# One row tile of every sixteenth pair fetched by SyncE, row by row, in a graph network kernel

## The reference

```
x = layernorm(x + three_graph_convolutions(x, src, dst))
bf  = exp(coeff * (dist[:, None] - centers[None, :]) ** 2)
bf  = ssp(ssp(bf @ W1 + b1) @ W2 + b2)
msg = h[src] * edge_feat * bf * cut[:, None]
agg = segment_prod(msg, dst)
x = layernorm(x + ssp(agg @ W3 + b3))
```

## Time and profile before

| what | value |
|---|---|
| median of 3 runs | 3990.79 us (3990.15 to 3992.11) |
| the profiled execution | 3993.41 us |
| its span, from first to last instruction | 3991.6 us |
| PE busy | 3243.2 us (81%) |
| DVE busy | 3237.0 us (81%) |
| ACT busy | 2862.5 us (72%) |
| POOL busy | 1935.5 us (48%) |

### The profile page before, as it was taken

How to read it: one execution, slowest core, us unless ns; L and a number is a source line. 1 busy time by engine, 2 the same in 40 slices (tenths; PEclk the granted TensorE clock), 3 DMA queues, 4 the chain that set the end, 5 groups by cost and what they waited for, 6 DMA issues and landing times. The chain is left out here.

```text
span 3991.6 us, 61034 instructions
## 1 busy us (share of the span) xinstructions
PE 3243.2 (81%) x21477; PEld 2658.1 (67%) x21477; DVE 3237.0 (81%) x5053; ACT 2862.5 (72%) x3091; POOL 1935.5 (48%) x1883
## 2 busy tenths in 40 slices
PE   5888888899999999999577777777777777777763
PEld 4777777778888888888466555555555555555552
DVE  8999999955554545455599999999999998999995
ACT  5666666554454445444699999999999999999974
POOL 6311200061220121022577777777777777777775
PEclk9898888899999999999888888888888888888885
DMA  5444434589999999999578877777777777777752
GB/s 156 150 140 150 152 125 133 175 278 325 320 310 312 313 312 312 317 328 319 170 217 217 217 216 210 210 211 212 214 209 212 207 211 207 211 212 210 209 164 77
DMA packets 369312, 883.06 MB, mean 221 GB/s; under 512 B 54843, under 2 KB 219952, under 8 KB 369016
## 3 DMA queue, kind: packets, MB, share of 16 engines
q1 hardware_dynamic: 277447, 742.20, 59.2%
q0 software_dynamic: 60928, 123.77, 13.2%
q10 hardware_dynamic: 30768, 15.26, 1.3%
HBM read 659.12 MB, written 221.89 MB: 221 GB/s over the span
## 5 line engine op out<-in xcount | busy, mean ns | idle before, releaser
L1270 POOL DMA_INDIRECT hgat<-x_rows,edge_src x1564 | 1476.1, 944 | 485.2 <-issue 475.8
L926 PE MATMUL psum<-wide,hp 128*128 128x490 f32 x4704 | 1062.5, 386 | 9.3 <-DVE wide L1016 8.0
L926 PEld LDWEIGHTS psum<-wide,hp 128*128 128x128 f32 x4704 | 886.4, 189 | 167.1 <-issue 8.5
L849 ACT CAST wide<-gran 128x1470 fp32r<-128x1470 bf16 x336 | 479.5, 1427 | 546.6 <-PE psum L926 546.4
L1016 DVE CAST wide<-gran 128x1960 fp32r<-128x1960 bf16 x336 | 398.6, 1187 | 424.3 <-PE psum L926 423.3
L610 PEld LDWEIGHTS psum<-hi_hot,lo_hot 128*128 128x128 bf16 x7840 | 545.8, 155 | 213.4 <-issue 64.3
L1451 DVE TENSOR_SCALAR psum<-rows_e,edge_same,edge_first 128x128 f32<-128x128 f32 x1564 | 646.1, 413 | 49.5
L520 ACT CAST gran<-psum 128x490 bf16<-128x490 f32 x784 | 451.6, 576 | 303.7 <-PE psum L610 292.9
L610 PE MATMUL psum<-hi_hot,lo_hot 128*128 128x49 bf16 x7840 | 574.1, 219 | 92.1 <-DVE hi_hot L397 90.2
L1375 PE MATMUL psum<-c_b,one_b 96*128 96x512 bf16 x391 | 187.8, 480 | 505.0 <-DVE prod_e L1433 501.5
L822 POOL DMA_INDIRECT x_sb<-h_rows,last_i x147 | 185.7, 1263 | 794.1 <-DMA h_rows<-h_out 743.6
(11 more groups left out here) (218 smaller groups left out, 3721.1 us busy)
## 6 DMA issues: line engine op xcount, KB each, us to landing
gran<-step_counts SPq DMA_DIRECT2D x336, 857.5 KB, 6.5
dist<-weight_by_step SPq DMA_DIRECT2D x195, 512.0 KB, 6.8
running_products<-rows_e SPq DMA_DIRECT2D x195, 512.0 KB, 3.2
step_counts<-gran SPq DMA_DIRECT2D x112, 857.5 KB
ef<-in_edge_attr SPq DMA_DIRECT2D x195, 448.0 KB
hgat<-x_rows,edge_src POOLq DMA_INDIRECT x1564
kn<-keep_and_norm_of_steps SPq DMA_DIRECT2D x48, 490.0 KB, 7.9
ef<-in_edge_attr SPq DMA_DIRECT2D x171, 64.0 KB
```

Of the source, the lines that this page charges most:

```text
L849: nc.scalar.copy(in_runs(i, NEAR, 7), by_tile(gran, i, NEAR, 7)).then_inc(s_wf, 1)
L926: last = nc.tensor.matmul(y, hps[:, 7 * g + t, part, :], wide[:, r, t, :], start=first, stop=last_)
L1270: pool.indirect_dma_start(out=hgat[:, f % U, c, :], out_offset=None, in_=x1_d, in_offset=bass.IndirectOffsetOnAxis(ap=edge_src[:, 2 * f + ...
```

## The change

For every sixteenth pair (f = 15, 31, ..., 191: twelve pairs, all of full width) POOL gathers seven row tiles and SP fetches the eighth. SP does it row by row: `value_load` reads one index of `edge_src` into a register of SP, with bounds 0 to N - 1, and a DMA of one row (512 bytes) with that register in its address brings the row to one partition of `row_of_sp`, of which there are two buffers. The 128 rows are spread over the SP loop: nine in each of the fourteen steps before, two in the fifteenth, none in the sixteenth (`A_TURN` = 9). They are issued at the head of a step, ahead of `load_dist`. DVE's product of such a pair is cut into one over seven row tiles and one over the eighth, which waits for the 128 rows (`s_spr`).

```diff
+            EVERY = 16
+            A_TURN = -(-P // (EVERY - 1))
+            by_sp = [f for f in range(PAIRS) if f % EVERY == EVERY - 1 and width(f) == PBLK]
+            row_of_sp = sbt("row_of_sp", [P, 2, D])
+            s_spr = [sem(f"s_row_of_sp{r}") for r in range(2)]
+            by_pool = lambda f: width(f) // P - (f in by_sp)
...
+                    def fetch_rows(f):
+                        q, turn = divmod(f, EVERY)
+                        if q < len(by_sp):
+                            if turn == 0 and q >= 2:
+                                sp.wait_ge(s_v, by_sp[q - 2] + 1)
+                            for p in range(turn * A_TURN, min((turn + 1) * A_TURN, P)):
+                                k = (by_sp[q] + 1) * C8 - 1
+                                row = sp.value_load(src_k[p:p + 1, k:k + 1], min_val=0, max_val=N - 1)
+                                sp.dma_start(row_of_sp[p:p + 1, q % 2, :], x1_d[bass.ds(row, 1), :]
+                                             ).then_inc(s_spr[q % 2], 16)
...
                     for f in range(PAIRS + 3):
+                        fetch_rows(f)
                         load_dist(f + Q)
...
-                        for c in range(width(f) // P):
+                        for c in range(by_pool(f)):
                             pool.indirect_dma_start(out=hgat[:, f % U, c, :], out_offset=None, in_=x1_d,
...
-                            dve.wait_ge(s_gt[f % U], 16 * (C8 * (f // U) + n))
+                            m = by_pool(f)
+                            dve.wait_ge(s_gt[f % U], 16 * sum(by_pool(i) for i in range(f % U, f + 1, U)))
...
-                            nc.vector.tensor_tensor(prod_e[:, f % R, 0:n], hgat[:, f % U, 0:n],
-                                                    ps2[f % 2][:, 0:n * D].rearrange("p (c d) -> p c d", d=D), ALU.mult
-                                                    ).then_inc(s_v, 1)
+                            last = nc.vector.tensor_tensor(prod_e[:, f % R, 0:m], hgat[:, f % U, 0:m],
+                                                           ps2[f % 2][:, 0:m * D].rearrange("p (c d) -> p c d", d=D),
+                                                           ALU.mult)
+                            if m < n:
+                                q = by_sp.index(f)
+                                dve.wait_ge(s_spr[q % 2], 16 * P * (q // 2 + 1))
+                                last = nc.vector.tensor_tensor(prod_e[:, f % R, m], row_of_sp[:, q % 2],
+                                                               ps2[f % 2][:, m * D:n * D], ALU.mult)
+                            last.then_inc(s_v, 1)
```

## The result

The changed kernel takes 4537.75 us (median of 4, 4537.08 to 4543.17) against 3990.71 (median of 4): 1.1373 of the time before, 95% interval 1.1359 to 1.1388, 547 us more. It is the second rival, B, at a price above the range, which ended at 4290.

The account below looks back on a forecast made before the run. POOL was taken as the bound at 9.99 us a pair; twelve gathers at 1.248 us save 15.0 us, with SP's rows fitting its idle time: 3990.8 - 15.0 = 3975.8 us, range 3972 to 4290.

Parts of the forecast that it names:

- B: Rival on SP: it becomes the bound in steps with nine rows, from 0.98 us a row; 4138 or more; chance 0.43.
- the sum of a row: On SP: load 0.23, three register instructions 0.27, DMA 0.32 and gap 0.04 make 0.86 us a row.
- the load: On SP: reading one index into a register, sized at 0.23 us from a one-element DMA's issue, bounded by 0.09 and 1.8.
- the signs it named for B: SP's waits for DVE gone, row DMAs back to back, ACT waiting for distances, POOL waiting for products.
- A: Product stage: rows fit in SP's idle time, POOL's saving of 15.0 us comes through, 3975.8 us; chance 0.48.
- its estimate of 377 us: Product stage: time added if a register load has a floor of about 600 ns, making a row 1.23 us.
- The register instructions: On SP: three for each row at 0.09 us each, 0.27 us together.
- The DMA of a row: On SP: issuing a one-row DMA takes 0.32 us, between 0.277 in quiet and 0.357 under load.
- POOL as the bound and the price of a gather: Product stage: POOL sets 9.99 us a pair; each gather costs 1.248 us, so twelve fewer save 15.0 us.
- DVE's split product: On DVE: cutting the product adds 0.15, perhaps 0.2 us in one pair of sixteen, within its 0.4 us of room.
- the formula: Product stage when SP sets the pace: longer by 12 x (128 x + 35.2 - 159.8) - 17 us, x a row's price.
- the slack of 17 us: SP's loads of distances: 23.8 us from issue to use less 6.8 landing, used once before SP's lateness shows.

Follow-up runs that it names:

- the load of twelve: Against the kernel before: every twelfth pair, indices turned into one partition, one load filling twelve registers, no bounds check; 3986.05 us, ratio 0.9976.
- the fixed row: Changed kernel with a fixed row number in place of the index read, row DMAs kept, no load or register instructions; 3982.67 us, ratio 0.9968.
- the kernel with the loads first: Changed kernel without the bounds check, a step's nine index loads placed first, then its nine row DMAs; 3984.15 us, ratio 0.9975.
- every twelfth pair: Changed kernel without bounds check, index loads behind the row DMAs of the step before, every twelfth pair in place of every sixteenth; 4063.07 us, ratio 1.0183.
- the best order found: Changed kernel without bounds check: distances and features, row DMAs, index loads for the next step, then the store; every sixteenth pair, 3978.72 us, ratio 0.9968.
- every thirteenth pair: Changed kernel without bounds check, index loads behind the row DMAs of the step before, every thirteenth pair in place of every sixteenth; 3975.42 us, ratio 0.9960.

## Why the prediction was wrong

**The step that failed** is the sum of a row, "0.23 + 0.27 + 0.32 + 0.04 = 0.86 us", and within it the load, taken as 0.23 from "the smallest DMA that SP issues". The step 0.86 stood 0.12 under the point from which SP decides; the row came to 1.34 on average. The prediction had rival B and its place right, and the signs it named for B are those that the profile shows; what it had wrong is the price that made A the likelier one.

**The load** took 0.50 us in the median, 0.58 on average and up to 2.1, against 0.23; the prediction took it from a DMA's issue and had no term for what stands ahead of it. Among other loads it takes 0.27 us, near to what was taken; right behind a row DMA it takes 0.50, and all but the first of a step had a row DMA right ahead. The second one of a step, the first row DMA and the store ahead of it, took 1.37 in the step shown and 1.14 on average:

```profile
L1266 SPq TENSOR_LOAD <-edge_src x1: 457/457/457, 3011.3 to 3011.3; - x1
...
L1266 SPq TENSOR_LOAD <-edge_src x2: 457/912/1367, 3011.3 to 3012.5; - x2
...
L1266 SPq TENSOR_LOAD <-edge_src x8: 490/502/1367, 3012.5 to 3022.6; - x8
```

So the order of loads and DMAs, not the load alone, decides: without the bounds check the interleaved order lost 133 us, and the grouped one gained 11. Of the two pages of the Trainium skill that the prediction set against each other, "DMA: Bandwidth & Descriptors" (section "Latency and other measured facts", a floor of about 600 ns) was nearer for this order, and its estimate of 377 us nearer to the 547, though no run shows a floor there: the shortest loads took 0.26 us. The 200 ns a register of "Runtime: NRT & Kernel Launch" (section "Instruction fetch mechanics") is nearer to the 0.27 of a load that stands among loads and to the 0.19 a register of the load of twelve.

**The register instructions** were taken as 0.09 each. Two of them were what the bounds check is made of, one of 152 ns; four, not three, stood in a row (the row of `ISA` in the order hides one), with gaps of 30 to 50 ns. They came to some 0.24 of instructions and 0.2 of gaps, against 0.27. This is the smaller half of the error, and the run without the check shows what the check is worth: 410 us. In that run all of a row but the load took less than the 0.63 us of the prediction (1.08 less a mean load of 0.61), and it was still 133 us slower: the load alone was enough to turn the forecast.

**The DMA of a row** was a little less than taken: 0.26 us against 0.32.

**POOL as the bound and the price of a gather** were right: with the fixed row, 12 gathers less gave 13 us of the 15, six gave 7 of 7.5, fifteen gave 16 of 18.7. The other kernels whose sum fitted gave less than their gathers too: 11 and 12 of 15 with the loads grouped, and 7 of 15 and 9 of 20 with the loss at the start. The shortfalls are within the intervals but for the 4 us of the kernel with the loads first, whose interval is 6 to 14 us less; why was not tried. **DVE's split product** was right: it costs nothing that shows.

**When rows don't fit**, the formula held in its slope (415 us expected from 0.27 us a row, about 410 found) and was off in its last term. With the measured 12.8 us a pair, 12 x (205 - 159.8) = 542 us against 547 measured: most of the slack of 17 us was not given back. From before to after the last load of distances moved from 3827.7 to 4380.2 (552.5 us) and the last store from 3897.5 to 4443.0 (545.5): only 7 were. With every twelfth pair the same two moved to 3914.5 and 3968.5, by 86.8 and 71.0, so there nearly all of it was. That the formula gives 12 x (128 x 1.34 + 35.2 - 159.8) - 17 = 546 with the measured row is therefore luck in part: SP's own work was 1.9 us a pair and not 2.2 (the two DMAs of features took 1.33 us right behind the store and the distances, 0.90 with the rows between), and the slack came back only in part. What decides how much of the slack comes back was not tried.

**The chances** gave B 0.43, but the range took in loads up to 0.55 us only, with all else as taken, and ended at 4290. The mean load of 0.58 alone, a row of 1.21, gives 4337 by the prediction's formula, and the register instructions, thought known, brought the rest.

## What to carry to other kernels

An engine that has 79% of its time idle is not free: price a new loop on it by the sum of all its instructions, the gaps and the checks that the language adds included, times the count, and compare with the idle time per round; here 0.1 us on a row was 154 us. Reading registers pays if the loads are grouped away from DMAs on the same queue and without bounds checks. Filling several registers from one instruction helped as well: with it twelve rows in a step fitted (3986 us), where twelve single loads in the best order found did not (4063 us). Its cost lay in laying out the indices at the stage's start; loads of several registers in that better order were not tried. Up to the limit the work costs nothing that shows and beyond it each part is paid in full, so leave a margin or measure at two sizes around it.

## What the runs showed of the hardware that was not expected

- A load of one word from on-chip memory into a register of SP took 0.27 us among other loads, 0.45 to 0.6 in most cases right behind a DMA of the same queue (once 1.28, with every thirteenth pair, behind a DMA of features and 2.3 us behind a store), and up to 2.1 us for the second to the fourth behind a store of 0.5 MB. Behind twelve DMAs of distances and features without a store, the second took 0.27. Behind the store, one load into nine registers took 3.07 us, one into twelve 2.31.
- A check of the bounds of a loaded value cost 0.27 us in the records: 152 ns and 18 ns and the gaps. Without it the mean row was 0.26 us shorter.
- Behind a DMA of 1536 single elements, the fourth DMA after it on the same queue took 7.5 us to issue, where it took 0.42 without it; with 2048 elements it took 6.2.
